# A perceiver block on one core: the first query chunk in products with the upper and with the lower weight parts, and the quantiser's parameters by ScalarE's queue

## What is computed

```
x = x + matmul(fake_quant(layernorm(x)), fake_quant(ctx))      # uint8 steps, scale and zero point from 4 parameters
h = layernorm(x)
q = h @ Wq                                                    # 2048 x 2048, 32 heads of 64
k, v = split(h @ Wkv)                                         # 2048 x 128, one key and value head for all
x = x + softmax(q k^T / 8 + alibi, causal) v @ Wo
x = x + layernorm(x) @ dequant4(qweight) + bias
```

## Time and profile before

| | |
|---|---|
| time, median of 3 runs | 431.39 us (430.06 to 432.17) |
| the profiled execution: its own time | 432.08 us |
| its span in the trace | 430.2 us |
| mean granted TensorE clock, of full speed | 0.98 |
| TensorE busy | 376.7 us (88%) |
| VectorE busy | 326.4 us (76%) |
| ScalarE busy | 220.5 us (51%) |
| GpSimd busy | 9.6 us (2%) |
| moved by the DMA engines | 77.43 MB |

### The profile page before, as it was taken

One profiled execution on the slowest core, in us unless ns is written; L12 is line 12 of the kernel. 1 busy time (PEld: TensorE's weight loads), 2 busy tenths in 40 slices (PEclk: granted clock), 3 DMA queues, 4 the chain that ended last, 5 costly groups with the idle time before them and its releaser, 6 DMA issues.

```text
span 430.2 us, 4695 instructions
## 1 busy us (share of the span) xinstructions
PE 376.7 (88%) x1830; PEld 279.9 (65%) x1836; DVE 326.4 (76%) x364; ACT 220.5 (51%) x266; POOL 9.6 (2%) x43
## 2 busy tenths in 40 slices
PE   0285577866999999999999989999799999999996
PEld 0121232323888887877877867888578878888884
DVE  4699788769941594794784965599999899999922
ACT  2967988896243395386474645535505233444000
POOL 6000000000000000000000001000000000000000
PEclk9999898999799999999999999999989999999999
DMA  7999999994072394393537321997100000000022
GB/s 278 425 421 421 419 424 422 417 393 187 2 270 94 136 233 159 131 246 117 192 99 277 114 98 34 312 314 292 69 2 1 2 0 0 2 0 2 0 98 98
DMA packets 24273, 77.43 MB, mean 180 GB/s; under 512 B 1626, under 2 KB 1802, under 8 KB 19210
## 3 DMA queue, kind: packets, MB, share of 16 engines
q1 hardware_dynamic: 24092, 77.01, 49.4%
q10 hardware_dynamic: 160, 0.13, 0.1%
HBM read 74.91 MB, written 2.10 MB: 179 GB/s over the span
## 4 chain that ended last, share of the span: by engine, by line
PE 65%; DVE 16%; DMA 8%; ACT 7%; issue 3%; SPq 0%; DVEq 0%; ACTq 0%
PE bank L1128 20%; PE bank L1001 10%; PE bank L1002 10%; PE bank L1003 10%; DMA ctx_more<-in_ctx 5%; ACT q L415 4%; DVE w_lo L624 3%; PE bank L962 2%; PE bank L1063 2%; DMA raw<-in_L_attn_Wo 2%; PE bank L994 2%; DVE stats L594 2%; PE bank L1088 2%; DVE q L676 2%; PE bank L1076 1%
## 5 line engine op out<-in xcount | busy, mean ns | idle before, releaser
L624 DVE TENSOR_TENSOR w_lo<-raw,w_hi 128x2048 fp32r<-128x2048 f32 x29 | 66.2, 2286 | 11.8 <-ACT w_hi L437 11.7
L437 ACT ACTIVATE w_hi<-raw 128x2048 fp32r<-128x2048 f32 x29 | 55.4, 1914 | 37.3 <-DMA raw<-in_L_attn_Wo 15.5
L1001 PE MATMUL bank<-w_hi,xt_hi 128*128 128x512 f32 x128 | 52.5, 410 | 0.0
L962 PE MATMUL bank<-q,at 128*128 128x512 bf16 x122 | 34.9, 405 | 19.8 <-DVE q L676 18.9
L1002 PE MATMUL bank<-w_lo,xt_hi 128*128 128x512 f32 x128 | 50.4, 394 | 0.0
L1003 PE MATMUL bank<-w_hi,xt_lo 128*128 128x512 f32 x128 | 50.3, 393 | 0.0
L676 DVE TENSOR_SCALAR q<-q 128x2048 bf16<-128x2048 uint8 x32 | 38.5, 1219 | 7.2 <-ACT q L415 4.5
L1001 PE MATMUL bank<-w_hi,hd_hi 128*128 128x512 f32 x104 | 41.1, 396 | 0.0
L1002 PE MATMUL bank<-w_lo,hd_hi 128*128 128x512 f32 x104 | 40.5, 390 | 0.0
L1003 PE MATMUL bank<-w_hi,hd_lo 128*128 128x512 f32 x104 | 40.5, 390 | 0.0
L462 ACT ACTIVATE work<-work,neg_mx 128x128 f32<-128x128 f32 x64 | 24.8, 390 | 25.0 <-DVE neg_mx L795 24.9
(11 more groups left out here) (152 smaller groups left out, 652.1 us busy)
## 6 DMA issues: line engine op xcount, KB each, us to landing
raw<-in_ctx SPq DMA_DIRECT2D x16, 1024.0 KB, 18.0
ctx_more<-in_ctx SPq DMA_DIRECT2D x16, 1024.0 KB, 17.9
raw<-in_L_attn_Wq SPq DMA_DIRECT2D x16, 1024.0 KB, 5.5
raw<-in_L_attn_Wo SPq DMA_DIRECT2D x13, 1024.0 KB, 5.2
raw_fifth<-in_L_attn_Wo SPq DMA_DIRECT2D x3, 1024.0 KB, 7.5
resid<-in_x SPq DMA_DIRECT2D x2, 1024.0 KB, 11.7
scale<-in_L_ffn_scales SPq DMA_DIRECT2D x16, 128.0 KB, 6.2
packed<-in_L_ffn_qweight SPq DMA_DIRECT2D x2, 1024.0 KB, 7.5
```

Of the source, the lines that this page charges most:

```text
L437: nc.scalar.activation(hi_slots[s], raw_slots[s], ACT.Copy).then_inc(w_hi_set, 1)
L624: nc.vector.tensor_tensor(lo_slots[s], raw_slots[s], hi_slots[s].bitcast(F32), ALU.subtract).then_inc(w_lo_set, 1)
L962: mm(bank[:, 4 * b + n, :], at[:, k, b * P:(b + 1) * P], q16[:, i % 2, n * CH:(n + 1) * CH], start=start, stop=False)
L1001: mm(bank[:, out_bank, :], x_hi, hi[:, c], start=first, stop=False)
```

## The change

It has four edits.

1. The four parameter loads move from the head of SP's list to the head of ScalarE's.
2. VectorE: the split of granule 0 moves from before batch 1's residual to behind its normalisation, where the split of granule 1 was; granules 1 to 3 follow behind the remainders.
3. ScalarE: the four upper parts of batch 1's transposed rows come before the upper part of the key and value weights.
4. TensorE: in chunk 0 `q_granule` is taken apart into `q_by_upper` (both parts of x with the upper weight part, 8 products, waits only for `w_hi`) and `q_by_lower` (the upper part of x with the lower weight part, 4 products, waits for `w_lo`). The order is new.

```diff
@@ block.sync
-            for i, p in enumerate((s1, z1, s2, z2)):
-                sp.dma_start(prm_row[0:1, i:i + 1], p.unsqueeze(0)).then_inc(prm_loaded, 16)
@@ block.scalar
+            for i, p in enumerate((s1, z1, s2, z2)):
+                act.dma_start(prm_row[0:1, i:i + 1], p.unsqueeze(0)).then_inc(prm_loaded, 16)
             act.wait_ge(eps_set, 1)
             nc.scalar.activation(warm[:], eps_col[:], ACT.Sqrt)
...
             sqrt_of(3)
+            for g in range(4):
+                upper(1, g)
             act.wait_ge(wkv_loaded, 16)
             act.wait_ge(at_done, B)
             nc.scalar.activation(kv_hi_t, kv_raw[:], ACT.Copy).then_inc(kv_hi_set, 1)
-            for g in range(4):
-                upper(1, g)
@@ block.vector
             colsums(1)
-            remainder_w(0)
             for n in range(NCH):
                 ins = first_residual(1, n)
             moments(1, ins)
             reciprocal_sd(3)
             normalise(1).then_inc(norm_set, 1)
-            remainder_w(1)
+            remainder_w(0)
             for g in range(4):
                 remainder(1, g)
-            remainder_w(2)
-            remainder_w(3)
+            for w in range(1, 4):
+                remainder_w(w)
@@ block.tensor
+            def q_by_upper(w, b):
+
+                pe.wait_ge(w_hi_set, w + 1)
+                pe.wait_ge(lo_out, 4 * (b + 1))
+                if b == 1:
+                    pe.wait_ge(resid1, B * NCH)
+                for x_part in (xt_hi, xt_lo):
+                    for t in range(4):
+                        k = 4 * (w - W_Q) + t
+                        mm(bank[:, Q_BANK[b], :], x_part[:, k, b * P:(b + 1) * P],
+                           hi_slots[slot_of(w)][:, t * CH:(t + 1) * CH], start=k == 0 and x_part is xt_hi, stop=False)
+
+            def q_by_lower(w, b):
+                pe.wait_ge(w_lo_set, w + 1)
+                for t in range(4):
+                    k = 4 * (w - W_Q) + t
+                    ins = mm(bank[:, Q_BANK[b], :], xt_hi[:, k, b * P:(b + 1) * P],
+                             lo_slots[slot_of(w)][:, t * CH:(t + 1) * CH], start=False, stop=k == KT - 1)
+                if b == B - 1:
+                    ins.then_inc(w_used, 1)
+                elif k == KT - 1:
+                    ins.then_inc(q_done, 1)
...
-            q_granule(0, 0)
+
+            for w in range(3):
+                q_by_upper(w, 0)
             transposes(1)
-            q_granule(1, 0)
-            q_granule(0, 1)
-            q_granule(1, 1)
-            q_granule(2, 0)
-            q_granule(2, 1)
-            q_granule(3, 0)
+            q_by_upper(3, 0)
+            q_by_lower(0, 0)
+            q_by_upper(0, 1)
+            q_by_lower(0, 1)
+            for w in range(1, 3):
+                q_by_upper(w, 1)
+                q_by_lower(w, 0)
+                q_by_lower(w, 1)
+            q_by_upper(3, 1)
             keys_values()
-            q_granule(3, 1)
+            q_by_lower(3, 0)
+            q_by_lower(3, 1)
             value_rows()
```

More of the change, by code:

```diff
@@ L1007, in q_granule @@
                 pe.wait_ge(w_lo_set, w + 1)
-                if n == 0:
-                    pe.wait_ge(lo_out, 4 * (b + 1))
-                    if b == 1:
-                        pe.wait_ge(resid1, B * NCH)
-                elif kq == 0:
+                if kq == 0:
                     pe.wait_ge(q_out, B * (n - 1) + b + 1)
```

## The result

The changed kernel takes **429.60 us** (median of 7 runs, 428.02 to 430.60) against 431.39 before (also seven runs). The ratio is 0.9952, 95% interval 0.9933 to 0.9970: faster by 0.5%, about 2 us, where 5.4 were predicted; 429.60 lies above the predicted range of 424.4 to 428.8. Its profiled execution took 428.70 us with a span of 426.8; the one of before took 432.08.

A forecast was written before the change was run, and what follows sets the result against it. Bound by the context's loads, VectorE's turn to the query projection, then nearly gapless TensorE; -1.24 - 1.16 - 2.73 - 1.16 + 0.8 = -5.5 us from the 431.39 median gave 425.9, stated as 426.0, range 424.4 to 428.8.

The forecast's parts named there:

- The turn: From context product to query projection: TensorE back at products at 109.2 instead of 110.38, 1.16 us gained.
- Twelve products fewer, and the clock: Behind the transposes: 72 products remain instead of 84, 2.73 us gained; clock stays up, another 1.16 us gained.
- Rival 1: At the transposes the clock falls all the same, costing 1.2 us: 427.2 us; chance 0.17.
- The far end: End of chunk 0: batch 0's query row copy lands behind the key/value products, so TensorE waits 0.8 us.
- the bound of 0: No added TensorE wait at the chunk's end, if the first issue overlaps the copy and the queue tightens up.
- Part A: Start: parameters by ScalarE's queue make x SP's first issue, 1.24 us gained, bounds -1.24 and 0.
- rival 3: Start: parameters queue behind the bulk, land near 20 us, some 13 us reach the end: 439 us; chance 0.05.
- the 3 us that VectorE was to have in hand: VectorE's waiting until 45.20, 1.90 us there and some 1.1 in short pieces, expected to absorb late parameters.
- rival 2: x lands as before, or a step between 45 and 92 us absorbs the early start: 427.1 us; chance 0.13.
- Rival 4: Residual still waits for zero-point products, or the chunk's-end wait is several us: under 2 us left, 430; chance 0.07.

The follow-up runs named there:

- experiment 6: The kernel before, plus four 4-byte loads into a row that nothing reads at the head of ScalarE's queue; 431.32 us.
- Experiment 3: The changed kernel, with VectorE's five parameter operations behind the statistics of x's first half, loads still on ScalarE's queue; 428.28 us, ratio 0.9897.
- experiment 9: The changed kernel plus four unused 4-byte loads on SP's queue in mid-program, ahead of the first output granule's load; 428.04 us.
- experiment 10: New product order, x first on SP's queue, parameters behind it there, x's statistics before the parameter wait; ratio 0.9873 to the kernel before, 0.9875 when repeated.
- experiment 2: The kernel before, with only its four parameter loads moved to the head of ScalarE's queue; 432.01 us, ratio 1.0009.
- experiment 5: The changed kernel plus four 4-byte loads into a row that nothing reads, at the head of SP's queue; 428.12 us.

## Where the prediction was right, and where it failed

By the timed runs the whole miss lies in the parameters' edit. The three others were reckoned at 1.16 + 2.73 + 1.16 - 0.8 = 4.25 us, and the order alone measured 3.8 and 4.5. The parameters' edit was reckoned at a gain of 1.24 us and cost about 2.1 on top of the order.

**The turn, right.** From the last conversion to the first product behind the transposes 1.61 - 0.41 = 1.20 us came off; predicted were 1.16. The pauses of 0.33 and 1.18 us were reckoned at 0.5 and 1.3.

**Twelve products fewer, and the clock, right.** 5.46 - 1.61 = 3.85 us came off behind it; predicted were 2.73 + 1.16 = 3.89. (72 products at full clock are 16.35 us by 72 x 0.22703, not 16.38, so the 1.16 should read 1.19.) From 100 us to the end of the chunk the clock stayed at 1.00 in all eleven traces with the new order (a fall between 92 and 100, at the end of stage 1, is in two of them), and it fell between 105 and 114 in all three with the old one. Rival 1, that it falls all the same, is out.

The trace of experiment 6's kernel, of the old order, takes the two terms apart. There the clock was back at 1.00 when the products began. From the start of batch 1's normalisation to granule 10's issue it took 162.05 us, 1.4 less than the 163.47 of before: 0.3 ahead of the first product and 1.1 behind it, for 1.16 reckoned. The new order takes 159.6 to 159.7 in all eleven traces, another 2.4 less: the twelve products' 2.73, less the 0.37 at the far end.

The stretch of 105.50 to 108.80 holds sixteen transposes and one product at 1.00. By the Trainium skill, page "TensorE: Matmul & The Clock Gate", section "Part 4: PE-mode transpose", transposes don't count as TensorE being busy in the way that products do. The fall that the prediction derived from it did not come. Whether transposes count is not settled. In experiment 6's trace TensorE's last product ends at 104.05, the clock falls at 107.5, from 108.00 on TensorE does transposes and nothing else, and the granted clock is back at 1.00 at 111.0, before the first product at 111.27. In the trace of before the same transposes, from 106.81 on, did not bring it back; it rose at 112.7, among the products.

**The far end, right in kind, too large.** The wait is 0.37 us and not 0.8. The step that failed is that ScalarE starts the issues at +1.71, behind the copy: the first issue started with the copy, at +1.13 (130.26, with the key and value products ending at 129.13). This was the bound of 0, "if the first issue overlaps the copy", partly taken.

**Part A, failed.** The step is that the fourth load lands between 3.2 and 4.5 us. The time from issue to landing was taken as 2.0 us or less from the earlier trace rows, a transfer with little beside it; with x ahead of it and the context behind it was 5.4. So VectorE was free at 9.0 and not at 4.8 to 6.1, and in the pair of traces the lead at the end of stage 1 was 0.4 us and not 1.24. I had set the point from which lateness costs something at 7.0 us, in rival 3, and gave it 0.05 since I thought only of the 17.9 us of a full tile. The landing came at 7.3, just beyond it: the rival's mechanism, with 7.3 in place of its 20. The Trainium skill, page "DMA: Bandwidth & Descriptors", section "Queues, rings and completion order", was cited there for DMA engines that take turns between the queues packet by packet. The wait of a mere packet that the prediction derived from it did not come; whether the engines took turns, no trace here shows.

What the late landing cost is less sure. By rival 3's own sum 7.3 would cost 0.3 us. Experiment 3, which takes the wait away and leaves granule 10 late, was 2.4 us faster than the changed kernel (about 0.9 to 3.9), so the 3 us that VectorE was to have in hand are probably too many. The traces can't fix it: the changed kernel, its repeat and experiment 9 are the same up to 190 us, and their last conversions come at 92.56, 91.50 and 94.08. On average the last conversion comes at 93.2 with the parameters on SP's queue ahead of x (six traces), at 92.6 with x first and VectorE held by late parameters (five), and at 91.8 with x first and the statistics ahead of the wait (three). That has the order that the account asks for, with differences smaller than the scatter.

Of rival 2 the first half is out: x landed at 5.6 to 5.8 in seven of the eight traces that issue it first, against 6.8 to 7.1. Whether a step between 45 and 92 us takes up a part of that is open; experiment 10's 1.3 us (about 0 to 2.5) speaks for little of it.

**Not in the prediction at all.** "Later loads, splits and softmax steps hang on TensorE's progress and move with it" failed at one load. Granule 10's issue moved with TensorE to 0.1 us, its landing didn't: +1.79 us. This is the larger part of the miss in the traces. In the pair of traces the miss is 5.5 - 3.4 = 2.1 us: 0.8 up to the end of stage 1 (of the size of its scatter), less 0.4 at the far end and 0.1 behind it, plus 1.8 from granule 10. That the parameters' edit is what makes the landing late is shown by experiments 2, 5 and 9; how it does is open. The remaining 1.6 us between the pair and the medians is the place of the two profiled executions in their own scatter, 0.7 and 0.9 us. I had allowed for the first.

Rival 4, that the order isn't what binds, gave the right number, 430, for the wrong reason: the order alone is worth 4 us.

## What to carry to other kernels

Take the landing time of a small transfer from one that has the same load beside it. Four bytes issued about a microsecond behind a megabyte were used 4.6 to 5.6 us after their issue on a queue of their own, and 4.1 us after it on the megabyte's queue; ahead of the megabyte 1.5 us were enough, on either queue. Put what is needed first at the head, and let an engine do what needs no parameters before it waits for them. And when a queue's list is changed, even by tiny loads, look at how long every later load on the chain takes to land, not only at when it is issued.

## What the runs showed of the hardware

- Four 4-byte loads more or fewer on SP's queue changed the landing of a 1 MB load up to 260 us later: 8.3 to 8.9 us with four ahead of it (eight traces), 10.3 to 10.7 with none or one (five traces). One of sixteen arrivals makes most of the difference.
- Four 4-byte loads, issued by 1.9 us on ScalarE's queue, were used at 3.36 when x's 1 MB was issued behind them (one trace), and at 6.5 to 7.5 when it was issued with the first of them (six traces). Behind x on SP's own queue it was 6.2 (two traces): a queue of its own did not help a small load here.
- While six loads to 16 partitions each were served, the DMA engines' share was 0.88 with 110 GB/s; with full tiles just before it was 1.07 with 394.
- With TensorE idle from about 104 us on, the granted clock fell between 105 and 108 in all three traces of the old order. In one of them it rose again while TensorE did only transposes (from 108.00, full clock at 111.0), in the other two only behind them.
- Two DMA issues on ScalarE's queue (1.16 us) and a copy of 0.60 us on ScalarE started at the same 130.26.
